# Turned tokens loaded and normalized by GpSimd, and values mixed for two tiles at a time, in the first stage of a two-layer kernel

## The reference

```python
x = x + cross_attention(_layernorm(x), ctx, ctx)     # 16 heads of 32, softmax, biases, Wo
x = x + expert_ffn(_layernorm(x))                    # 32 experts x 4 sets
x = x + mlstm_attention(_layernorm(x), ctx, ctx)     # 8 heads of 64
x = x + bitlinear_ffn(_layernorm(x))                 # ternary weights, 8-bit tokens

def _layernorm(x, axis=-1, eps=1e-05):
    m = jnp.mean(x, axis=axis, keepdims=True)
    v = jnp.var(x, axis=axis, keepdims=True)
    return (x - m) / jnp.sqrt(v + eps)
```

## Time and profile before

| | us |
|---|---|
| median of 3 runs | 2046.35 (2043.2 to 2050.53) |
| the profiled execution | 2044.19 |
| its span, first to last instruction | 2042.5 |
| PE busy in the span | 1749.6 (86%) |
| DVE, ACT, POOL busy | 1334.3, 1218.8, 604.1 |

### The profile page before, as it was taken

How to read it: one execution, slowest core, us unless ns; L and a number is a source line. 1 busy time by engine, 2 the same in 40 slices (tenths; PEclk the granted TensorE clock), 3 DMA queues, 4 the chain that set the end, 5 groups by cost and what they waited for, 6 DMA issues and landing times. The chain is left out here.

```text
span 2042.5 us, 40039 instructions
## 1 busy us (share of the span) xinstructions
PE 1749.6 (86%) x14608; PEld 1088.2 (53%) x14658; DVE 1334.3 (65%) x2641; ACT 1218.8 (60%) x2361; POOL 604.1 (30%) x1107
## 2 busy tenths in 40 slices
PE   6999999999999999999985886635689789789777
PEld 2666666666666666666652553214355455455443
DVE  2766757668577685866763564414687788788775
ACT  2676666666666666666661554412576876876765
POOL 1343124321233132332300000004455455455550
PEclk9999999999999999999987997667699999999889
DMA  7543435434356354443422659987336436334200
GB/s 236 137 130 87 148 103 153 131 97 152 101 131 173 87 167 125 114 135 96 125 71 94 200 162 374 408 296 260 116 118 209 131 117 211 129 117 159 82 26 31
DMA packets 167312, 303.19 MB, mean 148 GB/s; under 512 B 26128, under 2 KB 74320, under 8 KB 158800
## 3 DMA queue, kind: packets, MB, share of 16 engines
q1 hardware_dynamic: 126496, 214.48, 32.9%
q10 hardware_dynamic: 24240, 52.57, 7.6%
q0 software_dynamic: 16384, 33.59, 7.0%
HBM read 166.09 MB, written 67.34 MB: 114 GB/s over the span
## 5 line engine op out<-in xcount | busy, mean ns | idle before, releaser
L572 DVE TENSOR_REDUCE a_negmax<-a_score 128x1 f32<-128x512 f32 x512 | 347.1, 685 | 114.7 <-PE a_score L711 107.4
L453 ACT ACTIVATE a_prob<-a_score,a_negmax 128x512 f32<-128x512 f32 x512 | 353.7, 693 | 98.4 <-DVE a_negmax L572 98.0
L334 POOL DMA_DIRECT2D a_q_stack<-a_q_parts x512 | 251.2, 499 | 532.2 <-DVE a_q_parts L566 259.8
L711 PE MATMUL a_score<-a_k_stack,a_q_stack 128*128 128x512 f32 x512 | 358.1, 700 | 21.3 <-ACT a_prob L453 12.8
L719 PEld LDWEIGHTS a_turn<-a_ident,a_prob 128*128 128x128 f32 x2048 | 254.6, 141 | 137.3 <-issue 96.2
L719 PE MATMUL a_turn<-a_ident,a_prob 128*128 128x128 f32 x2048 | 309.9, 274 | 3.6 <-ACT a_perm L429 2.0
L342 DVE COPY a_probT<-a_turn 128x512 f32<-128x512 f32 x256 | 176.4, 689 | 201.9 <-PE a_turn L719 201.6
L342 ACT COPY a_probT<-a_turn 128x512 f32<-128x512 f32 x256 | 149.9, 586 | 251.1 <-PE a_turn L719 250.2
L711 PEld LDWEIGHTS a_score<-a_k_stack,a_q_stack 128*128 128x128 f32 x512 | 97.8, 191 | 138.3 <-issue 80.8
L2058 PE MATMUL c_ff<-c_w2T,c_hqT 128*128 128x512 bf16 x485 | 133.3, 431 | 44.3 <-ACT c_hqT L1651 42.1
L793 PE MATMUL a_work<-a_cT,a_Wk 128*128 128x512 f32 x256 | 132.4, 612 | 10.2 <-DMA a_Wk<-in_L_xattn_Wk 10.2
(11 more groups left out here) (205 smaller groups left out, 3050.0 us busy)
## 6 DMA issues: line engine op xcount, KB each, us to landing
a_k_stack<-a_k_parts SPq DMA_DIRECT2D x512, 64.0 KB, 2.7
a_q_stack<-a_q_parts POOLq DMA_DIRECT2D x512, 64.0 KB, 2.4
scratch_res<-b_chosen SPq DMA_DIRECT2D x32, 1024.0 KB, 9.7
c_res<-scratch_res SPq DMA_DIRECT2D x32, 1024.0 KB, 6.7
a_weights<-in_ffn_W ACTq DMA_DIRECT2D x16, 1024.0 KB, 4.9
c_negm<-scratch_m SPq DMA_DIRECT2D x64, 256.0 KB, 5.9
a_xs<-in_x ACTq DMA_DIRECT2D x8, 1024.0 KB, 6.0
a_x<-in_x ACTq DMA_DIRECT2D x8, 1024.0 KB, 6.0
```

What stands on the lines that cost most here:

```text
L334: eng.dma_start(stack[kind][i * DH0:(i + 1) * DH0, M % 2, g, :].bitcast(F32), parts[kind][g * DH0:(g + 1) * DH0, part, :].bitcast(F32)).th ...
L453: nc.scalar.activation(prob[:, U % 4, :], score.bank(U)[:, :], ACT.Exp, bias=negmax[:, u:u + 1], accum_out=sums[:, head_of(U), tile_of(U): ...
L572: nc.vector.tensor_reduce(negmax[:, U % UNITS:U % UNITS + 1], score.bank(U)[:, :], AX.X, ALU.max, negate=True).then_inc(max_ready, 1)
L711: nc.tensor.matmul(score.bank(U)[:, :], stack["Q"][:, M % 2, g, t * P:(t + 1) * P], stack["K"][:, M % 2, g, :], start=True, stop=True).the ...
```

## The change

It has two parts. **Tokens:** the host also gives x turned (`x_T`, features on the partitions). It is loaded into `xT` as it is, 1 MB a batch, at u = 28. DVE puts mean and inverse root of the 512 tokens side by side (`norm_cols`, 128x8, u = 21); PE turns that (`NM`, u = 23, an 8x128 result), ACT copies it, stores it to DRAM, and at u = 26 loads it back to all partitions (`norm_rows`, 512 KB). POOL then subtracts and multiplies `xT` in place, two instructions of 128x2048 between the stack of group 3 and the residual. Q of the next batch waits for that. `xn`, the 16 transposes, DVE's four results and ACT's four copies are gone. For batch 0 DVE does both instructions, and Q comes last of the first products. **Values:** `probT` is a ring of ten places instead of two times four, and `mix_values` runs for two tiles in one step, at every eighth g (10, 18, ...).

```diff
+    SLOTS = 2 * HM + 2
...
-    FIRST_TURNS = [("XT", 0, c) for c in range(C)]
-    FIRST_PRODUCTS = [("K", 0, 0), ("V", 0, 0), ("V", 0, 1), ("Q", 0, 0), ("V", 0, 2), ("V", 0, 3), ("K", 0, 1)]
-    STATS_AT, SCALE_AT, RESULT_AT = 13, 17, 21
+    FIRST_TURNS = [("NM", 0, 0)]
+    FIRST_PRODUCTS = [("K", 0, 0)] + [("V", 0, t) for t in range(T)] + [("K", 0, 1), ("Q", 0, 0)]
+    STATS_AT, SCALE_AT, COLUMNS_AT, ROWS_AT = 13, 17, 21, 26
...
-        probT = sb("probT", [P, 2, HM, T, P])
+        probT = sb("probT", [P, SLOTS, T, P])
...
                     for m in (1, 2, 3):
                         stack_parts(pool, "Q", b * GROUPS + m)
+                    if b + 1 < B:
+                        pool.wait_ge(xT_in, (b + 2) * 16)
+                        pool.wait_ge(norm_in, (b + 2) * 16)
+                        row = lambda k: norm_rows[:, k, :].unsqueeze(1).to_broadcast([P, C, S])
+                        nc.gpsimd.tensor_tensor(xT[:, :, :], xT[:, :, :], row(0), ALU.subtract).then_inc(pool_chain, 1)
+                        pool.wait_ge(pool_chain, b + 1)
+                        nc.gpsimd.tensor_tensor(xT[:, :, :], xT[:, :, :], row(1), ALU.mult).then_inc(xT_ready, 1)
...
+                act.dma_start(xT[:, :, :], A["x_T"][0]).then_inc(xT_in, 16)
...
+                    if kind == "NM":
+                        if b:
+                            act.wait_ge(norm_stored, b * 16)
+                        nc.scalar.copy(norm_turned[:, :], turn.bank(j)[0:2 * T, 0:P]).then_inc(turn.free[j % 2], 1)
+                        turn.wait_read(act, 0, j)
+                        act.dma_start(scratch["norm"][b], norm_turned[:, :]).then_inc(norm_stored, 16)
+                        return
...
+                def load_norm(b):
+                    act.wait_ge(norm_stored, (b + 1) * 16)
+                    if b:
+                        act.wait_ge(xT_ready, b)
+                    act.sem_inc(act_parted, 1)
+                    act.dma_start(norm_rows[:, :, :].rearrange("p k s -> p (k s)"),
+                                  scratch["norm"][b].rearrange("k p -> (k p)").partition_broadcast(P)).then_inc(norm_in, 16)
...
+                    if u == ROWS_AT and b + 1 < B:
+                        load_norm(b + 1)
+                    if u == C * 7 and b + 1 < B:
+                        work.wait_full(act, 0, jobs["Q", b, GROUPS - 1])
+                        act.dma_start(xT[:, :, :], A["x_T"][b + 1]).then_inc(xT_in, 16)
...
-                norm0.on_vector(dve, chain, xs, xn).then_inc(xn_ready, 1)
...
+                norm_columns(0)
                 low("K", 0, 0)
+                dve.wait_ge(xT_in, 16)
+                dve.wait_ge(norm_in, 16)
+                row = lambda k: norm_rows[:, k, :].unsqueeze(1).to_broadcast([P, C, S])
+                chain.step(nc.vector.tensor_tensor(xT[:, :, :], xT[:, :, :], row(0), ALU.subtract))
+                nc.vector.tensor_tensor(xT[:, :, :], xT[:, :, :], row(1), ALU.mult).then_inc(xT_ready, 1)
...
-                        if RESULT_AT <= u < RESULT_AT + T:
-                            last = norm0.tile_result(xs, xn, u - RESULT_AT)
...
+                        if u == COLUMNS_AT:
+                            norm_columns(b + 1)
...
-                                                    probT[:, q % 2, g, k, :], start=k == 0, stop=k == T - 1, skip_group_check=True)
+                                                    probT[:, (q * HM + g) % SLOTS, k, :], start=k == 0, stop=k == T - 1, skip_group_check=True)
...
-                    if rest == 0 and 0 <= q < ALL // HM:
+                    if rest == 0 and q % 2 == 1 and 0 <= q < ALL // HM:
+                        mix_values(q - 1)
                         mix_values(q)
```

More of the change, by code:

```diff
@@ L567, in low, with norm_columns @@
                                                    parts[kind][:, 0, :].bitcast(F32), ALU.add, ALU.subtract).then_inc(work.free[j % 2], 1)
+                def norm_columns(b):
+                    if b:
+                        turn.wait_full(dve, 0, entries["NM", b - 1, 0])
+                    nc.vector.tensor_copy(norm_cols[:, 0, :], norm0.mv[:, :, 0])
+                    chain.step(nc.vector.tensor_copy(norm_cols[:, 1, :], norm0.rstd[:, :]))
+                    dve.sem_inc(norm_ready, 1)
                 def maximum(U):
@@ L631, in _ @@
                 dve.wait_ge(x_in, 16)
-                norm0.on_vector(dve, chain, xs, xn).then_inc(xn_ready, 1)
-                dve.wait_ge(xn_ready, 1)
+                for t in range(T):
+                    last = norm0.tile_stats(xs, t)
+                norm0.moments(dve, chain, last)
                 dve.sem_inc(xs_read, 1)
+                norm0.scale(chain)
+                norm_columns(0)
                 low("K", 0, 0)
+                dve.wait_ge(xT_in, 16)
[3 more added lines that the diff above has]
+                nc.vector.tensor_tensor(xT[:, :, :], xT[:, :, :], row(1), ALU.mult).then_inc(xT_ready, 1)
                 low("Q", 0, 0)
@@ L754, in turn_tiles @@
                         return
-                    if kind == "XT" and n == 0:
-                        pe.wait_ge(xn_ready, b + 1)
-                    elif kind == "NT" and n == 0:
+                    if kind == "NM":
+                        turn.wait_free(pe, 0, j)
+                        pe.wait_ge(norm_ready, b + 1)
+                        nc.tensor.transpose(turn.bank(j)[0:2 * T, 0:P], norm_cols[:, :, :].rearrange("p k t -> p (k t)"),
+                                            ident[:, :]).then_inc(turn.full[j % 2], 1)
+                        return
+                    if kind == "NT" and n == 0:
                         pe.wait_ge(xn1_ready, b + 1)
@@ L775, in product @@
                     if 0 in steps:
-                        turned = {("Q", 0): "XT", ("L", 0): "NT"}.get((kind, n))
+                        turned = {("L", 0): "NT"}.get((kind, n))
                         if turned:
@@ L779, in product @@
                                 turn.wait_read(pe, 0, entries[turned, b, c])
+                            pe.sem_inc(pe_parted, 1)
+                        if kind == "Q" and n == 0:
+                            pe.wait_ge(xT_ready, b + 1)
                             pe.sem_inc(pe_parted, 1)
@@ L801, in _ @@
                     product("V", 0, t, range(C))
-                for c in range(C):
-                    turn_tiles("XT", 0, c)
-                pe.wait_ge(wq_ready, 2)
-                product("Q", 0, 0, range(C))
+                turn_tiles("NM", 0, 0)
                 for t in range(T // 2, T):
@@ L809, in _ @@
                 product("K", 0, 1, range(C))
+                pe.wait_ge(wq_ready, 2)
+                product("Q", 0, 0, range(C))
                 for U in range(AHEAD):
@@ L2118, in laid_out @@
         "gate_biases": biases.reshape(T * 32, 2),
+        "x_T": inputs["x"].reshape(B, S, C, P).transpose(0, 3, 2, 1),
         "ctx_T": ctx.reshape(B, S, C, P).transpose(0, 3, 2, 1),
```

36 lines of the change are left out of this document (17 added, 19 removed).

## The result

The changed kernel takes 2075.97 us (median of 4 runs, 2070.03 to 2089.89), the kernel before 2047.72 in the runs beside it: ratio 1.0153, interval 1.0114 to 1.0193. It is slower by some 28 us where +5 was predicted, and outside the range of 2031 to 2067. The profiled execution took 2070.03 us, 25.8 more than that of before.

The account below looks back on a forecast made before the run. It took PE to bound most of the first stage, DVE u = 36 to 42. Start +8.5, batch 0 -3.1, batches 1 to 6 +0.6, batch 7 -0.7 gave +5.3: 2050 us, range 2031 to 2067.

Parts of the forecast that it names:

- The second mixing: Values, in the loop: a pair's second mixing follows without idle time, saving 0.38 us a pair, 24 us for all 64.
- the hold: Inverse root, batches 1 to 6: DVE waits for POOL's running instruction, 1.7 us a batch; bounds 0 and 3.8.
- Batches 1 to 6 without the hold: Loop outside u = 35 to 42: pairs, less a small turn and two sums taken off, save 1.6 us a batch.
- the turns inside u = 35 to 42: Loop: PE would lose 2.2 us with half a pair's idle, but DVE's work there stays; saving put at 0.
- They start when the stack of group 3 has been issued: POOL's two instructions, batch 2: start at 360.40, take 10.1 us, end at 370.5.
- the sum of the start: Before the first scores: a chain ahead of Q and a new product bank wait cost +8.5 us; bounds +3, +14.
- last link: Start: first stack issued by 50.6, last DMA landed about 2.4 us later, 53.0, with the loads ahead nearly through.
- The shared product bank: Start: Q of group 1 waits for the low part of K, 2.25 us and some 0.5 more.
- the stage's end: Very end of batch 7: two tiles are mixed where one was, +0.8 us.
- D: Rival: pairs don't merge, each mixing keeps its 1.22 us, turns saved only in batch 0; +22, 2069 us; chance 0.09.
- C: Rival: POOL runs at its longest rate, 12.2 us for both, hold 3.8 in six batches; +17.9, 2064 us; chance 0.18.
- A: Rival: PE bounds the stage all the way and POOL does no harm; -18, 2028 us; chance 0.12.

Follow-up runs that it names:

- e4: The changed kernel with POOL's two instructions of 128x2048 cut into eight of 128x512: 2077.98 us, ratio 1.0161.
- e7: e3_loads_late with batch 0's tokens as in the kernel before and POOL's two instructions ahead of its stack of group 3: 2050.12 us, ratio 1.0018.
- e9: e7 with POOL's two instructions also waiting for DVE's widening copy of unit 32: 2035.25 us, ratio 0.9942.
- e5: The kernel before with the ring of ten and paired mixing alone, tokens normalized in place, next x load at unit 46: 2041.79 us, ratio 0.998.
- e11: e10 with four of a batch's sixteen tiles mixed one at a time, the other twelve in pairs: 2018.47 us, ratio 0.9851.
- e12: e5 with e10's late start loads and e11's four single mixings, tokens turned by PE: 2022.32 us, ratio 0.9878.
- e3_loads_late: The changed kernel with the loads of x and ctx for the batch after next at unit 34 instead of 26: 2056.49 us, ratio 1.0053.
- e10: e9 with the start's loads of batch 1's x and the experts' first weights issued behind the third exponential: 2028.74 us, ratio 0.991.

## Why the prediction was wrong

*Right.* The second mixing follows without idle: 0.34 a pair, 0.38 said. The mechanism of the hold, its place and its end with POOL's instruction: shown by e4, e7 and e9. POOL at 4.54 us an instruction (5.05 said). Batches 1 to 6 without the hold: -1.67 us on average in e9_pool_between, -1.6 said. That is luck in part, since the -1.6 had two errors against each other: the pairs alone keep 0.76 (e5), as two of eight cost instead of saving, and the turns inside u = 35 to 42 gave 1.2 (e11 against e12) where 0 was put.

*The step that failed first* is "They start when the stack of group 3 has been issued", with batch 2's row standing for all six batches. POOL also waits for `x_T`, whose load was not followed: issued at u = 28 behind 2 MB on the same queue, it landed after 12.7 us in the median. For it POOL started 2.0, 1.4, 6.1 and 2.7 us late in batches 1, 2, 4 and 5; in batch 6, with no load ahead of it, it landed after 5.4 us and POOL was on time. In batch 3 the stack itself was late. There the trace of the kernel before already has only 6.4 us from the end of POOL's last issue (493.26) to the inverse root (499.65), where batch 2 has 9.2; POOL issued at 485.35 what had been ready since 482.08, and no trace shows what for.

The hold, said to be 1.7, was 2.7, 2.2, 3.3, 6.4, 3.4 and 0.8: 18.7 us in six batches (from the lengths of L144 and L146 less 0.16 and 0.17) instead of 10.2. It splits up. POOL's two instructions took 9.2 us together, not 10.1; with that the prediction's own sum gives 0.8 a batch, as e3_loads_late shows it in five of the six; for six that is 4.6. Batch 3's late stack adds 2.6, and the lateness of `x_T` 11.5, which e3_loads_late takes out. The prediction gave the upper bound of 3.8 to a slow POOL; it was a late one. e9_pool_between takes out what is left.

*The second* is the sum of the start, 8.5 for 14.4. By its links: store issued 24.02 (23.3 said), landed by 30.8 (29.3), rows back at 34.13 (32.3), tokens done 38.85 (37.1), Q over 5.37 instead of 3.67, because PE's granted clock, after an idle of 3.35 us, was 0.50 (the 1.2 GHz level) between 39 and 42; low part done 45.82, POOL's last issue over 54.14 (50.6), landed 58.07 (53.0). That last link assumed that 2 MB put ahead of the stack would be through by then; x landed at 49.9, the weights at 54.4. The sequence of waits was right, and DVE's two instructions and the way from Q's end to POOL's first issue took what was said. Put short were the store's issue by 0.7, its landing by 0.8, the rows by 0.3, Q by 1.7 and the last link by 1.5: 5.1 together. The shared product bank cost 2.45 (2.75 said). The unit behind it is 1.1 longer: PE was busy throughout it in both traces, 6.58 us at a mean granted clock of 0.75 (62.95 to 69.53) where 5.49 at 0.89 stood before (49.62 to 55.11), and both products are 4.9. So it is the same work at a lower clock, behind PE's 2.11 us of idle for the bank.

*Put short:* the stage's end, +2.4 for 0.8. The last pair stands alone on the path, and the granted clock is 0.67 on average between 1087 and 1092; its 64 loads take 2.80 where 1.69 is usual:

```profile
1087.95 2.80 PEld L784 LDWEIGHTS a_mix<-a_probT,a_v 128*32 128x32 f32 x64 [0.33 <-issue]
```

In e4, e7, e9 and e11 the same 64 loads take 1.69 (in e9 at a granted clock of 1.00), and the end costs 0.9, as said. What decides between the two isn't shown: PE's waits of 1.16, 0.25 and 1.64 us ahead of the pair are the same in e9 as here.

The +3.4 behind the stage are no effect of the change that the runs could show: the code there is the same in all kernels, and from the last load of Wo's weights to the end the traces have between 959 and 967 us (960.0 before, 963.4 here). Of the rivals D (2069) stands nearest, and is wrong: the pairs merge. C (2064) had the right kind of cause, a longer hold, with the wrong reason for it. Against A stand PE's 8.5 us of freed time in 140, which came to nothing in this kernel. With the waits out of the way (e11) the time is 28 us below the kernel before, some 6.5 of them from the two loads moved at the start, which are no part of the change.

## What to carry to other kernels

When work moves to an engine that stands idle, ask for each of its inputs when it lands, loads included, and what stands ahead of them in the queue: a long instruction that starts late collides with other work than the one planned for. Read its start in every batch, not in one: a batch that is late for a reason of its own is in the trace beforehand. An instruction of one engine can hold up another's without any semaphore between them; list which of the neighbour's instructions can be held (the list below), and put the long one in a gap by a wait (e9), rather than cut it up (e4) or only move it (e7). Merging small pieces of work pays where the engine is the bound, and costs where one of the pieces was hidden: choose place by place.

## What the runs showed of the hardware

- While a GpSimd tensor_tensor of SBUF operands runs, some DVE instructions between SBUF operands wait for its end, however short they are themselves: the copy of 128x512, the tensor_scalar of 128x4 (float and int32), and tensor_tensor and scalar_tensor_tensor of 128x4 with two SBUF inputs. 0.16 became up to 3.58 (batch 5) and 0.17 became 4.34. The small ones end 0.02 to 0.03 us behind GpSimd's, the copy 0.28 to 0.29. Others did not lengthen: maxima and copies out of PSUM, additions with one PSUM input, and, though they work from SBUF to SBUF, bn_stats, bn_aggr and reciprocal. The Trainium skill ("SBUF — State Buffer", Who interferes with whom) calls the shared ports an exclusive lock that whoever issues first keeps for the whole instruction, for two-port modes and for two SBUF inputs; the traces agree where GpSimd was first.
- 1 MB took 5.5 us to land behind nothing and 12.7 behind 2 MB of its own queue; the last six 64 KB DMAs of the first stack landed 5.7 to 8.8 us after their issue in the kernel before, with 2 MB of loads issued amid them, and 1.8 to 2.0 without (e10).
